# Order of the softmax normalisation of two heads at the end of each head pair, on eight NeuronCores

## What is computed

```python
xn = _layernorm(x, axis=-1)
# attention (one shared k and v of width 128)
q = (xn @ Wq).reshape(b, s, 32, 128)
kv = xn @ Wkv
k, v = (kv[..., :128], kv[..., 128:])
scores = jnp.einsum('bqhd,bkd->bhqk', q, k) * 128 ** -0.5
scores = jnp.where(causal, scores + slope[h] * (pos_k - pos_q), -jnp.inf)
attn = jax.nn.softmax(scores, axis=-1)
s = jnp.einsum('bhqk,bkd->bqhd', attn, v).reshape(b, s, h) @ Wo
# gate
w = qweight.astype(jnp.float32) * scales + scaled_zeros
g = _silu(jnp.einsum('bsi,oi->bso', xn, w.reshape(O, I)) + bias)
x = x + s * g
```

## Time and profile before

| | us |
|---|---|
| median of three runs | 7665.45 |
| the three runs | 7562.03, 7997.0, 7665.45 |
| the profiled execution | 7551.37 |
| span of its slowest core (core 1) | 7549.8 |
| spans of the eight cores | 7506.0 to 7549.8 |
| mean granted clock of TensorE | 0.821 to 0.823 |

### The profile page before, as it was taken

One profiled execution on the slowest core, in us unless ns is written; L12 is line 12 of the kernel. 1 busy time (PEld: TensorE's weight loads), 2 busy tenths in 40 slices (PEclk: granted clock), 3 DMA queues, 4 the chain that ended last, 5 costly groups with the idle time before them and its releaser, 6 DMA issues.

```text
span 7549.8 us, 55896 instructions; the slowest of 8 cores (7506.0 to 7549.8 us)
## 1 busy us (share of the span) xinstructions
PE 4348.8 (58%) x18152; PEld 1763.1 (23%) x18152; DVE 2472.5 (33%) x2572; ACT 1820.4 (24%) x2712; POOL 1017.4 (13%) x787
## 2 busy tenths in 40 slices
PE   0000545666896220066566996995665668969930
PEld 0000212222343220011111443441111113434410
DVE  4443001111002442267676000006785782000012
ACT  6775000000001440034244000013462461000000
POOL 0000000000000000034344000003562561000000
PEclk9999987888997555577677998997787789989965
DMA  8777777777444779800000435440000002354578
GB/s 273 293 299 250 143 143 146 152 156 156 105 96 134 213 212 294 293 0 1 28 1 12 98 93 114 115 105 27 1 1 28 1 1 67 98 108 111 114 201 281
DMA packets 1553326, 936.98 MB, mean 124 GB/s; under 512 B 1331602, under 2 KB 1487250, under 8 KB 1520018
## 3 DMA queue, kind: packets, MB, share of 16 engines
q1 hardware_dynamic: 1243794, 648.17, 34.4%
q10 hardware_dynamic: 309248, 285.24, 11.9%
HBM read 581.01 MB, written 251.66 MB: 110 GB/s over the span
## 4 chain that ended last, share of the span: by engine, by line
PE 44%; DVE 22%; DMA 21%; ACT 6%; issue 3%; SPq 3%; POOL 1%; DVEq 0%; ACTq 0%; POOLq 0%
PE pbE L779 12%; PE pbE L829 11%; PE pqC L475 9%; DVE accA L674 9%; DVE rd_f L740 6%; DMA wqrC<-wq 4%; DMA xA<-xkv 3%; DMA wobh<-wobD 3%; DMA xntB<-xnh 3%; DMA xcF<-xq 3%; PE pbE L735 3%; ACT wfoD L544 3%; PE pbE L694 2%; DVE stA L300 2%; PE pbfD L564 2%
## 5 line engine op out<-in xcount | busy, mean ns | idle before, releaser
L475 PE MATMUL pqC<-xntqC,wqbC 128*128 128x512 bf16 x4096 | 936.0, 393 | 340.3 <-DVE wqbC L456 284.1
L674 POOL TENSOR_TENSOR accA<-accA,ppb 128x512 f32<-128x512 f32 x719 | 978.1, 1360 | 178.0 <-ACT ppb L719 50.3
L829 PE MATMUL pbE<-attnTE,wftslE 128*128 128x512 bf16 x4096 | 888.8, 380 | 125.4 <-DMA wftslE<-wfth 124.4
L719 ACT ACTIVATE ppb<-pbE,bslE 128x512 bf16<-128x512 f32 x1264 | 779.9, 695 | 739.6 <-PE pbE L694 664.9
L674 DVE TENSOR_TENSOR accA<-accA,ppb 128x512 f32<-128x512 f32 x681 | 870.4, 1278 | 229.7 <-ACT ppb L719 96.3
L779 PE MATMUL pbE<-attnTE,woslE 128*128 128x512 bf16 x4096 | 887.8, 380 | 18.2 <-DMA woslE<-wobh 18.2
L694 PE MATMUL pbE<-qtsE,kt 128*128 128x512 bf16 x1528 | 582.7, 438 | 378.9 <-DMA tsbE<-tstk 378.9
L669 POOL CAST accA<-ppb 128x512 f32<-128x512 bf16 x64 | 39.1, 612 | 5073.1 <-ACT ppb L724 3190.7
L379 PE MATMUL pbigB<-xntB,wkv_bf 128*128 128x512 bf16 x384 | 162.6, 423 | 878.3 <-DMA xntB<-xnh 872.1
L663 PE MATMUL pbE<-ppb,vt 128*128 128x512 bf16 x1528 | 572.7, 405 | 145.6 <-ACT ppb L719 103.5
L475 PEld LDWEIGHTS pqC<-xntqC,wqbC 128*128 128x128 bf16 x4096 | 409.2, 100 | 867.1 <-issue 418.6
(11 more groups left out here) (51 smaller groups left out, 2822.6 us busy)
## 6 DMA issues: line engine op xcount, KB each, us to landing
xA<-xkv SPq DMA_DIRECT2D x48, 2048.0 KB, 10.6
xnh<-xnA ACTq DMA_DIRECT2D x64, 1024.0 KB, 10.8
wqrC<-wq SPq DMA_DIRECT2D x32, 2048.0 KB, 19.2
qwD<-qw SPq DMA_DIRECT2D x32, 2048.0 KB, 8.8
worD<-wo SPq DMA_DIRECT2D x32, 2048.0 KB, 16.6
woslE<-wobh SPq DMA_DIRECT2D x64, 1024.0 KB, 8.9
wftslE<-wfth SPq DMA_DIRECT2D x64, 1024.0 KB, 8.5
xA<-xq SPq DMA_DIRECT2D x16, 2048.0 KB, 11.6
```

Of the source, the lines that this page charges most:

```text
L475: mm_done = P.emit("tensor", lambda e, jj=j, c_=ch, p_=pb: e.matmul(pq[:, 2048 * p_ + 512 * c_:2048 * p_ + 512 * (c_ + 1)], wqb[p_][:, 128 ...
L674: ac = P.emit(eng, lambda e, pi=ppi_p, i_=i_p: e.tensor_tensor(out=accA[:, 512 * i_:512 * (i_ + 1)], in0=accA[:, 512 * i_:512 * (i_ + 1)], ...
L719: ex = P.emit("scalar", lambda e, b_=sb, pi=ppi, f_=fi, j_=j: e.activation(ppb[:, 512 * pi:512 * (pi + 1)], pb_[b_][:], AF.Exp, bias=bsl[: ...
L829: bb=bkf: e.matmul(pb_[bb + qq][:], wftsl[p_][:, 128 * g_:128 * (g_ + 1)], b_[:, c_ + 512 * qq:c_ + 512 * (qq + 1)], start=(g_ == 0), stop ...
```

## The change

At the end of a pair, the six operations of head 0 are no longer all emitted ahead of those of head 1. First come both sums (L735), then both reciprocals, then both casts. The spread, the copy and the multiply stay in one loop, head by head. The guards of the buffers move with their operations; both casts wait for the last L747 of the pair before. The second wait of L747, for the reciprocal, goes; the wait for the cast, which comes later on the same engine, stays.

```diff
                     flush_avd()
+                    dmms = {}
+                    rcs = {}
+                    rcbs = {}
+                    for i in range(2):
+                        dmms[i] = P.emit("tensor", lambda e, i_=i: e.matmul(
+                            pb_[6 + i_][0:1, :], c_onecf[:], accA[:, 512 * i_:512 * (i_ + 1)],
+                            start=True, stop=True),
+                            waits=[last_ac[i], bank_free[6 + i]], incs=[("t", 1)])
+                        acc_guard[i] = ("t", dmms[i])
+                    for i in range(2):
+                        rcs[i] = P.emit("vector", lambda e, i_=i: e.reciprocal(
+                            out=rd_f[i_][:], in_=pb_[6 + i_][0:1, :]),
+                            waits=[("t", dmms[i]), ("v", rcb_guard[i])], incs=[("v", 1)])
+                    for i in range(2):
+                        rcbs[i] = P.emit("vector", lambda e, i_=i: e.tensor_copy(
+                            out=rd_b[i_][:], in_=rd_f[i_][:]),
+                            waits=[("v", rcs[i]), ("t", rmm_guard)], incs=[("v", 1)])
+                        rcb_guard[i] = rcbs[i]
                     prev_mul = 0
                     for i in range(2):
                         h = heads[i]
-                        dmm = P.emit("tensor", lambda e, i_=i: e.matmul(
-                            pb_[6 + i_][0:1, :], c_onecf[:], accA[:, 512 * i_:512 * (i_ + 1)],
-                            start=True, stop=True),
-                            waits=[last_ac[i], bank_free[6 + i]], incs=[("t", 1)])
-                        acc_guard[i] = ("t", dmm)
-                        rc = P.emit("vector", lambda e, i_=i: e.reciprocal(
-                            out=rd_f[i_][:], in_=pb_[6 + i_][0:1, :]),
-                            waits=[("t", dmm), ("v", rcb_guard[i])], incs=[("v", 1)])
-                        rcb = P.emit("vector", lambda e, i_=i: e.tensor_copy(
-                            out=rd_b[i_][:], in_=rd_f[i_][:]),
-                            waits=[("v", rc), ("t", rmm_guard)], incs=[("v", 1)])
-                        rcb_guard[i] = rcb
                         rmm = P.emit("tensor", lambda e, i_=i: e.matmul(
                             pb_[6 + i_][:], c_oner[:], rd_b[i_][:],
                             start=True, stop=True),
-                            waits=[("v", rcb), ("v", rc)], incs=[("t", 1)])
+                            waits=[("v", rcbs[i])], incs=[("t", 1)])
                         rmm_guard = rmm
```

## The result

| | us |
|---|---|
| changed kernel, median of 10 runs | 7431.2 (7384.27 to 7877.28) |
| kernel before, median of 10 runs | 7778.13 (7562.03 to 8048.74) |
| ratio of the comparable runs, 95% interval | 0.973 (0.964 to 0.982) |
| profiled execution, after / before | 7421.8 / 7551.37 = 0.983 |

The change makes the kernel faster; whether by more than 2% the interval of the whole times leaves open. That is 158 us or 2.1%, ratio 0.979.

A forecast was written before the change was run, and what follows sets the result against it. No engine is full; DVE and PE wait in turns in 64 head-pair tails per core. Restart savings of 30.6 + 17.4 + 31.9 + 31.5 + 5.1 and 2.9 at slot ends give 119.4 us: 7551.4 to 7432, range 7385 to 7545.

The forecast's parts named there:

- Which order, and who waits for whom: Pair tail: PE released 2.55 us earlier, DVE 1.45; head 1's PV then waits for the second multiply; other stages unchanged.
- The second sum behind POOL costs nothing: PE queue: second sum, now before the first broadcast, waits for POOL's last accumulate; priced at nothing, 1.5 us of margin.
- the list of DVE times: Tail operations on DVE timed from the first reciprocal, about 0.09 us between two; next scores at 8.46, second multiply over at 11.22.
- the cost of the late PV: L663 of head 1 waits for the later multiply, holding the next scores: 0.37 us late in 8 restarts, 0.80 in 18.
- near, both heads: Restarts of near-head pairs where both heads start together: PV is free, 2.55 us saved in each of 12, 30.6 us.
- near, head 1 alone: Restarts of near-head pairs that head 1 begins alone: PV 0.37 us late, 2.18 us saved in each of 8, 17.4 us.
- far, head 1 alone: Restarts of far-head pairs that head 1 begins alone: PV moves with the second multiply, 1.45 us in each of 22, 31.9 us.
- far, both heads: Restarts of far-head pairs begun by both: head 1's PV 0.80 us late, 1.75 us saved in each of 18, 31.5 us.
- to query block 1: Passage from query block 0 to 1: loads wait for PE's count alone, 2.55 us saved in each of 2, 5.1 us.
- The waits of PV: L663's waits for the multiply at L757: up from 22 to 48, about 50 us in all instead of 10.2.
- POOL beside copy and multiply: POOL's first copies overlap DVE's copy1 and mul1: no stretching, both stay 0.69 us; stretching was a rival, 7462 us, chance 0.10.
- The rival with the full gain everywhere: All 62 restarts gain 2.55 us because the pair absorbs the late PV: 161 us, 7390 us, chance 0.15.

The follow-up runs named there:

- chained kernel: Changed kernel with waits added, each one-partition operation but the first waiting for the one directly ahead; four attention stretches 2027.9 us, 37 more than the changed kernel.
- casts-in-loop kernel: Sums and reciprocals of both heads first, each cast in the loop with spread, copy, multiply; four attention stretches 2085.0 us, 63.4 less than before.
- order kernels: Changed kernel, last loop head 1 first: always, stretches 1997.9 us; only where head 1 alone begins the next pair, 1976.0 us; changed kernel 1990.7.

## Why the prediction was right or wrong

The time stated, 7432, is the measured median to a microsecond, and that is luck: it was a gain 38 us too small, taken from an execution faster than most. As a forecast of the change it failed: I held "within 2%" to be likeliest (0.76) and gave faster by more 0.20; it was 2.1% faster by the undisturbed dies, 2.7% by the comparable runs (1.8 to 3.6).

- *Which order, and who waits for whom:* right. PE goes on first, DVE follows, PV meets the late multiply; nothing outside the attention stretches moved.
- *The second sum behind POOL costs nothing:* right. The second reciprocal has no wait in any of 64 tails; the 64 waits left at L742 are for the first sum.
- *The step that failed is the list of DVE times,* in the words "each with the gap of the same neighbours ... (about 0.09 between two instructions)". 0.09 is the gap between a reciprocal and its own cast, which waits for it. R1 waits for nothing on DVE, C0 for R0 and C1 for R1, so that each has an unrelated operation directly ahead. The term measured: R1 at 3.27 instead of 3.44, C0 at 6.48 for 6.88, the spread at 6.98 for 7.45, the next scores at 7.92 for 8.46, the second multiply over at 10.74 for 11.22. PE's release is 3.09 us earlier and not 2.55, DVE's 1.93 and not 1.45. Put into the sum of the prediction: 12 x 3.09 + 8 x 2.66 + 22 x 1.93 + 18 x 2.23 + 2 x 3.09 + 2 x 1.93 = 151 us, of 158 measured. This alone reaches the 151 us that I had set as the limit of 2%. The chained kernel shows it the other way round: with these gaps back the gain is 120.5.
- *The trace of before had the row.* In far restarts an unrelated DVE instruction follows a multiply directly; timeline of DVE, kernel before:

```profile
3503.67 0.69 DVE L757 TENSOR_TENSOR attnTE<-pbE,rs_f 128x512 bf16<-128x512 f32 x1
3504.28 0.42 DVE L669 CAST accA<-ppb 128x512 f32<-128x512 bf16 x1
```

3503.67 + 0.69 = 3504.36, and the next one has started at 3504.28. Independent neighbours overlap by 0.08 where dependent ones stand 0.09 apart, 0.17 for each. I read the tail closely and took its gap, but not this row.
- *The other 7 us lie in the cost of the late PV, which was put too high where both far heads start and where near head 1 starts alone.* Gains in us of each restart, from one tail's first reciprocal to the next one's, mean of eight cores (the two tails that end a slot have none):

| restart | times | forecast | with the measured tail | measured |
|---|---|---|---|---|
| near, both heads | 12 | 2.55 | 3.09 | 3.16 |
| near, head 1 alone | 8 | 2.18 | 2.66 | 2.92 |
| far, head 1 alone | 22 | 1.45 | 1.93 | 1.91 |
| far, both heads | 18 | 1.75 | 2.23 | 2.46 |
| to query block 1 | 2 | 2.55 | 3.09 | 3.34 |

- *The waits of PV:* right in number and total, 47 and 49.0 us for 48 and about 50, but the total hides errors that cancel. On core 1 the 22 far restarts of head 1 alone wait 1.64 us each (1.45 and more forecast), 17 far ones of both heads 0.65 (0.8), the 8 near ones 0.23 (0.4). With the measured tail the forecast waits would be 0.86 and 0.43 in the last two kinds; 0.2 less in 26 restarts is 5 of the 7 us. The casts-in-loop kernel, which gains 9 us more than its tail, has them in the same two kinds (1.2 us each where its tail gives 0.9). Why PV is held 0.2 us less there, no run shows. The order kernels showed that the late PV costs time, less per restart than I had put on it.
- *POOL beside copy and multiply:* right. All 128 copies and all 128 multiplies after take 690 to 693 ns, and on core 1 they overlap POOL's work in 99 places, 29 us in all. POOL's copy takes its usual 0.61 in this restart (timelines of POOL and DVE, after):

```profile
3457.32 0.61 POOL L669 CAST accA<-ppb 128x512 f32<-128x512 bf16 x1 [11.25 <-ACT ppb L719]
```
```profile
3456.44 0.69 DVE L758 COPY rs_f<-pbE 128x512 f32<-128x512 f32 x1
3457.24 0.69 DVE L763 TENSOR_TENSOR attnTE<-pbE,rs_f 128x512 bf16<-128x512 f32 x1
```

The rule that the prediction took from the Trainium skill, "SBUF — State Buffer", "Who interferes with whom", agrees with these rows.
- *The rival with the full gain everywhere* (161 us) is near the measured 158 by chance: its mechanism, PV's wait absorbed, is not what the restarts show: the 22 far ones of head 1 alone gain 1.91 us, where the near ones of both heads gain 3.16. A number that comes out near a rival's does not make the rival true.
- *The chances.* The range for whole times was wide enough because of the scatter of executions. The range of the mechanism, 7405 to 7450, stood for the clock; the gap between instructions, which 64 tails multiply by three neighbours each, was not in it. 0.17 us x 3 x 64 is 33 us, the difference between 1.6% and 2%. The measured gain taken off the profiled execution, 7551 - 158 = 7393, lies outside that range.

## What to carry to other kernels

When a change interleaves two dependent chains on one engine, price the neighbours anew: take the start-to-start distance of instructions that don't wait for one another, not the gap inside the chain. In a chain of small operations that hands over to another engine, the place of the last small one (here a cast of some 0.4 us) sets when that engine goes on. And before reordering a slow operation, ask what its time depends on: laid out as 128x4 instead of 1x512, and with the heads ordered, the reciprocal took off another 336 us, where the reordering had taken off 158.

## What the runs showed of the hardware that I had not expected

- A VectorE operation that waits for the one directly ahead of it starts about 0.1 us after that one's shown end; one that waits for nothing or for an earlier one starts 0.08 us ahead of it. Start to start, two reciprocals of 1x512 stand 3.45 us apart with the wait (chained kernel) and 3.27 without, in all tails; two casts together take 0.93 and 0.68. It isn't only so on one partition: the 128x512 multiply and the cast behind it show the same 0.08. The Trainium skill, "VectorE: DVE Perf Modes", "The DRAIN you can't avoid", says of eight copies that "the semaphore costs nothing extra here", and also that "A next op that is not held starts earlier", that is, one that isn't made to wait for those ahead. The rows agree with the second sentence; for these operations the first doesn't hold, and the measurement decides.
- The reciprocal's time goes by columns for each partition, in the three shapes measured: 3.35 us for 1x512 and for 128x512, 0.18 for 128x4.
- A cast of 1x512 shows 0.41 us where it stands behind its own reciprocal, and two of them 0.68 together where neither waits for the one directly ahead.
